# A scan layer with experts: the order of two products in GpSimd's queue

## What is computed

```
xr = rmsnorm(x) @ W_in ; xs, res = split(xr)            # 512 + 512 channels
xs = silu(conv(xs, 4 taps) + conv_b)
dt, B, C = split(xs @ W_x) ; dt = softplus(dt @ W_dt)
A_disc = exp(A * dt)          # per channel and state: 512 x 16
Bx     = dt * B * xs
h[t]   = A_disc[t] * h[t-1] + Bx[t]
y[t]   = sum over 16 states of h[t] * C[t]
out    = residual + (y * silu(res)) @ W_out
```

## Time and profile before

| | us |
|---|---|
| median of 3 runs | 2591.76 |
| lowest, highest | 2589.58, 2592.09 |
| the profiled execution | 2596.7 |
| its span in the trace | 2594.9 |

### The profile page before, as it was taken

One profiled execution on the slowest core, in us unless ns is written; L12 is line 12 of the kernel. 1 busy time (PEld: TensorE's weight loads), 2 busy tenths in 40 slices (PEclk: granted clock), 3 DMA queues, 4 the chain that ended last, 5 costly groups with the idle time before them and its releaser, 6 DMA issues. The chain is left out here.

```text
span 2594.9 us, 22594 instructions
## 1 busy us (share of the span) xinstructions
PE 1693.1 (65%) x5652; PEld 663.2 (26%) x5652; DVE 1991.6 (77%) x2517; ACT 1234.5 (48%) x1908; POOL 2012.7 (78%) x666
## 2 busy tenths in 40 slices
PE   5775857677676858585958586777767684441580
PEld 2221322222222313131313222222222231110580
DVE  1059797989888898989797989898888889975212
ACT  2245455555555555555455555555555554431121
POOL 0048888897988888888888888989798888970456
PEclk9887988888897979796979898888889796655795
DMA  2083333434343424343323334343434333302762
GB/s 93 17 227 72 94 90 90 91 97 91 98 91 91 96 71 93 78 95 89 87 71 95 84 90 99 89 91 98 91 97 91 82 85 85 91 17 74 249 183 70
DMA packets 135471, 245.20 MB, mean 94 GB/s; under 512 B 25536, under 2 KB 77514, under 8 KB 135232
## 3 DMA queue, kind: packets, MB, share of 16 engines
q1 hardware_dynamic: 129472, 233.83, 36.3%
q0 software_dynamic: 5888, 10.29, 1.7%
HBM read 78.92 MB, written 31.13 MB: 42 GB/s over the span
## 5 line engine op out<-in xcount | busy, mean ns | idle before, releaser
L768 DVE TENSOR_TENSOR_SCAN h<-pa,carry,bq 128x512 f32<-128x512 f32 x1024 | 1261.4, 1265 | 169.9 <-ACT pa L622 149.7
L891 POOL TENSOR_TENSOR h<-h,c_rep 128x2048 f32<-128x2048 f32 x256 | 1157.0, 4529 | 221.3 <-DVE carry L773 221.3
L622 ACT ACTIVATE pa<-rep,neg_a 128x512 f32<-128x512 f32 x1024 | 690.4, 685 | 522.3 <-DVE h L768 518.5
L884 POOL TENSOR_TENSOR bq<-rep,b_rep 128x2048 f32<-128x2048 f32 x128 | 579.3, 4526 | 62.8 <-DVE h L768 51.4
L382 PE MATMUL pp<-mid,w_c 128*128 128x512 f32 x1024 | 484.2, 614 | 42.3 <-ACT xs L547 27.2
L360 PE MATMUL py<-h,blk 128*32 128x512 f32 x2048 | 330.3, 699 | 216.4 <-POOL h L891 122.9
L404 PE MATMUL pp<-xs,w_dtx 128*128 128x512 f32 x512 | 281.1, 695 | 120.4 <-ACT gate L552 106.2
L754 DVE TENSOR_TENSOR bq<-rep,pb 128x2048 f32<-128x2048 f32 x128 | 289.1, 2259 | 11.5 <-PE pb L413 11.5
L382 PEld LDWEIGHTS pp<-mid,w_c 128*128 128x128 f32 x1024 | 185.3, 191 | 328.4 <-issue 243.6
L389 PE MATMUL pp<-mid,w_res 128*128 128x512 f32 x256 | 153.9, 731 | 94.5 <-DVE du L694 56.4
L547 ACT ACTIVATE xs<-pp,cb 128x512 f32<-128x512 f32 x64 | 44.0, 688 | 288.0 <-PE pp L382 288.0
(11 more groups left out here) (155 smaller groups left out, 1621.2 us busy)
## 6 DMA issues: line engine op xcount, KB each, us to landing
rep<-du SPq DMA_DIRECT2D x1024, 128.0 KB, 2.4
c_rep<-bc_scratch SPq DMA_DIRECT2D x64, 256.0 KB, 4.7
combine_scratch<-zeros SPq DMA_DIRECT2D x16, 520.0 KB, 8.4
xt<-in_L_attn_x_dram SPq DMA_DIRECT2D x16, 512.0 KB, 3.6
b_rep<-bc_scratch SPq DMA_DIRECT2D x64, 128.0 KB, 2.8
mid<-in_L_attn_x_dram SPq DMA_DIRECT2D x16, 512.0 KB, 3.5
out_dram<-z SPq DMA_DIRECT2D x16, 512.0 KB, 3.2
hidden_scratch<-hid SPq DMA_DIRECT2D x16, 512.0 KB, 2.9
```

The source lines that it names most:

```text
L622: act.activation(pa[:, decay_bank(t), :], rep[:, c % 2, t % 4, 0, :], ACT.Exp, scale=neg_a[:, a_column(t):a_column(t) + 1]).then_inc(s_exp, 1)
L768: v.tensor_tensor_scan(h[:, quad % 4, t % 4, :], pa[:, decay_bank(t), :], bq[:, quad % 2, t % 4, :], carry[:, par, t:t + 1], ALU.mult, ALU ...
L884: pool.tensor_tensor(bq[:, 1], rep[:, c % 2, :, 1, :], b_rep[:, g // 2, :].unsqueeze(1).broadcast_to((P, 4, T)), ALU.mult).then_inc(s_bp, 1)
L891: pool.tensor_tensor(h[:, quad % 4], h[:, quad % 4], c_rep[:, par, quad % 4, :].unsqueeze(1).broadcast_to((P, 4, T)), ALU.mult).then_inc(s ...
```

## The change

In GpSimd's `step`, the input product of slots 0, 8, ..., 56 is moved behind the product of states of the same slot. The instructions and what each waits for are the same; only their order in GpSimd's queue differs, in 8 places of a tile.

```diff
                 def step(i, par, has_late, has_prev, has_cur, has_next, has_second):
                     for t in range(UNITS):
-                        if t % 8 == 0 and has_cur:
-                            inputs(t // 4 + 1, i)
                         if t == 0 and has_prev:
                             states(QUADS - 1, i - 1, 1 - par)
                         elif t % 4 == 0 and t > 0 and has_cur:
                             states(t // 4 - 1, i, par)
+                        if t % 8 == 0 and has_cur:
+                            inputs(t // 4 + 1, i)
                         if has_late:
                             post(UNITS + t, i - 2, par)
```

## The result

The changed kernel takes 2782.2 us (median of 4 runs, 2780.79 to 2787.39) against 2591.93 us before. The ratio is 1.0732, 95% interval 1.0705 to 1.0759: 190 us slower. The direction was as forecast, and so was the chain that holds the even quads; the size was not.

A forecast was written before the change was run, and what follows sets the result against it. VectorE and GpSimd handing work to each other bound the kernel, with all waiting in even quads. Floor 183 (187 - 3.7) + 45 + 22 + 9 = 259, added to the median 2591.76: 2850 us, range 2785 to about 2905.

The forecast's parts named there:

- The chain and its floor: Even quads: save, states product, input product, first scan form a closed chain of 10.49 us; odd quads keep 63.54 a tile.
- Quad 2, +45: Quad 2, around ScalarE's SiLU block and TensorE's chunk 3: 3.0 us over the floor in 15 tiles, +45 us.
- the clock term: In quad 2, TensorE idles 5 to 6 us before chunk 3; some six matmuls at slower pace add about 2.5 us.
- Quad 6, +22: Quad 6: slot 25's second tiny VectorE operation may wait for GpSimd's port, 2.9 us over the floor; even odds, +22 us.
- Quads 8 and 10, +9: Quad 8's own excess and that of quad 10 over the 10.49 us chain: 0.3 us each, +9 us.
- The tail, -3.7: Behind the last scan: GpSimd's last owed product starts with the final save, not about 3.7 us after it: -3.7 us.
- Floor 187: Scan loop: chain and odd quads, less first and last tiles' savings, give 2344.4 against 2157.4 us: +187 us.
- a case that had 0.03: Rival, even quads: neither term above the floor bites, 2775 us; chance 0.03 below 2785.
- Slack: Rival: GpSimd so far behind that both operands are there when it comes; time stays at 2592 us; chance 0.03.
- the faster side: Rival: odd states 4.5 us sooner free TensorE and ScalarE's decays; VectorE's 149.7 us waits going whole give 2442; chance 0.02.
- Quad 9: Rival: slot 36's second tiny operation waits for the port in quad 9, 68 us, 2918 us or more; chance 0.09.
- its threshold: Faster rival: wins if the chain is under the even quads' mean of 9.13 us, a product of 3.85 us, not 4.53.

The follow-up runs named there:

- e1: Changed kernel, with each VectorE carry save issued ahead of the next quad's first scan: 2801.14 us.
- e8: Changed kernel, with the 128x4 operations moved from VectorE to GpSimd and each carry save ahead of the next quad's first scan: 2706.16 us, ratio 1.0405.
- e10: Changed kernel, with GpSimd's states product on 256 of 512 columns (half of that work left out): 2620.13 us.
- e7: Changed kernel, with the 128x4 additions and negations moved from VectorE to GpSimd: 2787.9 us, ratio 1.0718.
- e9: Order of before, with GpSimd's states product on 256 of 512 columns (half of that work left out): 2545.39 us.
- e2: Order of before, with states first in slot 32 alone: 2538.12 us, ratio 0.9794.
- e4: Order of before, with states first in slots 0, 8, 32 and 40 alone: 2559.57 us, ratio 0.9879.
- e3: Order of before, with states first in slots 16, 24, 48 and 56 alone: 2802.07 us, ratio 1.0813.
- e11: Order of before on GpSimd, with each carry save ahead of the next quad's first scan: 2673.25 us, ratio 1.0287.

## Why the prediction was right and where it failed

**The chain and its floor: right.** The forecast put the tiles at 2344.4 us by 10.49 for each even quad and VectorE's own work for each odd one; they measure 2344.71. That it fits to 0.3 us is luck: sixteen full tiles of 147.66 are 3.2 us more than forecast, and the first and last tiles fall 2.9 us further short of full ones (the last quad, for one, takes 3.7 us and not 7). Save to states' start is 0.21 (1113.28 to 1113.49), states to inputs 4.47. e1 and e8 shorten the chain by a scan, e10 by half a product, and the quads follow. That is shown, not only argued. The odd quads kept their length within 0.3 us in sum, as forecast.

**Quad 2, +45: wrong, and the largest error.** The step that failed is "Chunk 2 is emptied in slot 4, now about 0.7 into quad 1". ScalarE, emptying chunk 1 in the kernel before (chunks 2 and 3 are in rows 9):

```profile
973.37 0.69 ACT L547 ACTIVATE xs<-pp,cb 128x512 f32<-128x512 f32 x1 [5.14 <-PE pp L382]
```

and chunks 1 to 3 in the changed kernel:

```profile
1037.18 0.69 ACT L547 ACTIVATE xs<-pp,cb 128x512 f32<-128x512 f32 x1 [3.32 <-PE pp L382]
...
1046.52 0.69 ACT L547 ACTIVATE xs<-pp,cb 128x512 f32<-128x512 f32 x1 [2.54 <-PE pp L382]
...
1055.63 0.69 ACT L547 ACTIVATE xs<-pp,cb 128x512 f32<-128x512 f32 x1 [0.26 <-PE pp L382]
...
1063.75 1.91 ACT L622 ACTIVATE pa<-rep,neg_a 128x512 f32<-128x512 f32 x3
```

and TensorE:

```profile
1047.26 5.42 PE L382 MATMUL pp<-mid,w_c 128*128 128x512 f32 x12 [0.86 <-ACT xs L547]
```

Quad 1's first scan started at 1047.6 (its save at 1048.77, less 1.2), and chunk 2 was emptied 1.1 ahead of it (0.4 to 1.9 in tiles 1 to 14), not 0.7 behind it. With that, the forecast's own sum gives -1.1 + 17.96 - 6.96 = 9.9, less than the chain's 10.49. What ScalarE needs from VectorE to reach slot 4 is a bank that the last scan of quad 0 frees, and the scans of quad 0 are done in its first 5 us. The wait that ended last was for TensorE's convolution, 2.54 us, and that started when chunk 1 had been emptied: 9.34 us from chunk 1 to chunk 2, before (973.37 to 982.71) and now. I had let ScalarE wait for the start of quad 1, which is where VectorE waits and not where ScalarE does. An engine two units ahead of the one that is held uses the hold: from chunk 2 to chunk 3 it took the same 9.11 us as before, TensorE stood idle 0.86 us and not 5 to 6, and the clock term had no ground (the grant was 1.00 in quads 0 and 2 above). The block ended in time for quad 3, with little to spare: from chunk 3 to that scan 9.41 us passed, and it needs 8.85. Quad 2 has 10.51 as its median.

**Quad 6, +22: wrong.** The first of the tiny pair waits to the end of the states product, as forecast; the second always slipped into the gap:

```profile
1096.33 2.65 DVE L719 TENSOR_SCALAR mean<-mv 128x4 f32<-128x4 f32 x1
1098.90 0.16 DVE L720 TENSOR_SCALAR var<-mv 128x4 f32<-128x4 f32 x1
```

Of the 32 of its kind the longest took 0.167 us, 15 of them directly behind a first one that had waited. I had taken even odds from rows 11; here the position against GpSimd's product is the same in every tile, so it is one outcome 15 times, not a mean of two. e7 confirms that the port's share is nothing.

**Quads 8 and 10, +9: wrong, but small.** They read 10.61 and 10.51.

**The tail, -3.7: smaller.** The span behind the last save fell by 0.85 us (276.40 to 275.55). The last states product doesn't start with the final save but 1.0 behind it, because it follows another product in GpSimd's queue. VectorE's last gating came 2.9 us sooner after that save; 2.1 of it were lost again later, most of it in the experts' part of the span, and why stays open.

**The median.** Floor 187 and these small ones give 186 in the profiled executions (2780.8 - 2594.9); the medians differ by 190, because the profiled execution of before lies 4.8 above its median and the other 0.4. All three terms above the floor came to nothing or nearly so, a case that had 0.03. They weren't independent: each assumed that something in an even quad needs more than 10.5 us, and a quad made 2 to 5 us longer has room for just such things.

**The other rivals.** Slack didn't absorb the change; the faster side didn't occur for the whole change, and e9 and e10 refute its threshold. Quad 9 kept its 7.11. What the order gives by itself is the port wait of quad 8, and e2 collects it.

## What to carry to other kernels

When two engines hand work to and fro, write down for each queue place what the instruction waits for, and add up the closed chain it makes: a product that must wait for a fresh result, put ahead of one that doesn't, brings its wait into both. Compare that chain with each stretch by itself, not with the mean: the same swap made five quads 3.7 to 5.2 us longer and quad 8 4.0 shorter, and quad 2 fell by 4.9 largely because the quads ahead of it had grown (in e4 quad 2 gave back just the 3.7 that quad 0 took). Once a stretch is held by such a chain, other terms in it are hidden until they pass it; add them only after following each engine to the event that it itself waits for.

## What the hardware showed unexpectedly

Whether a 128x4 VectorE operation takes 0.16 us or 3.5 to 4.5 hung on its start against a GpSimd product: 0.02 to 0.03 us ahead of it, it passed; 1.1 us behind its start, it waited to the end. What came directly behind one that had waited mostly slipped in ahead of GpSimd's next product: over five traces (before, e1, e3, e9, e11) the first operation of slot 32 waited 70 times; the second then took 0.16 us 62 times, and the third waited, and 8 times it was the second that waited. Moving a 0.13 us save ahead of a 1.28 us scan thereby cost 7.1 us in a pair of quads. The Trainium skill's page "SBUF — State Buffer", section "SBUF: two separate sides", has it that whoever starts first holds the shared ports for the whole instruction; these rows agree.

The clock showed just as sharply: in one run (e4) the same four matmuls took 1.98 us at a granted clock of 1.00 in some tiles and 3.78 at 0.50 in others, and quad 15 took 6.96 or 9.8 us with them.
